# Self attention in a decoder layer: queries scaled at their eviction, row maxima written straight as the exponentials' bias

## The reference

```python
q = (x @ Wq).reshape(b, t, 2 * H, HD).transpose(0, 2, 1, 3) * HD ** (-0.5)   # H = 16, HD = 16: a quarter
k = (x @ Wk).reshape(b, t, 2 * H, HD).transpose(0, 2, 1, 3)
v = (x @ Wv).reshape(b, t, H, 2 * HD).transpose(0, 2, 1, 3)
aw = softmax(einsum('bhqd,bhkd->bhqk', q, k) + causal)
aw = aw.reshape(b, H, 2, t, t);  aw = aw[:, :, 0] - lam * aw[:, :, 1]
attn = einsum('bhqk,bhkd->bhqd', aw, v)      # then an RMS norm over each head and attn @ Wo
```

## Time and profile before

| | us |
|---|---|
| median of 3 runs | 3828.13 |
| lowest, highest | 3823.77, 3829.65 |
| the profiled execution | 3817.57 |
| span of its trace | 3815.8 |

### The profile page before, as it was taken

One profiled execution on the slowest core, in us unless ns is written; L12 is line 12 of the kernel. 1 busy time (PEld: TensorE's weight loads), 2 busy tenths in 40 slices (PEclk: granted clock), 3 DMA queues, 4 the chain that ended last, 5 costly groups with the idle time before them and its releaser, 6 DMA issues.

```text
span 3815.8 us, 74126 instructions
## 1 busy us (share of the span) xinstructions
PE 3668.1 (96%) x24778; PEld 2905.2 (76%) x24778; DVE 2883.4 (76%) x5969; ACT 2352.5 (62%) x5418; POOL 1812.3 (47%) x2121
## 2 busy tenths in 40 slices
PE   6999999789999999999899999999999999999999
PEld 6888888534444444444589999999999999999998
DVE  5888888578888888888457777777777777777333
ACT  5888888457777777777435555555555555555121
POOL 2333332334555555554326666665666665555210
PEclk9999999789999999999899999999999999999999
DMA  5000000133334444443149999999999999998421
GB/s 209 24 25 28 27 26 21 42 108 123 127 124 133 133 128 127 131 154 121 48 141 265 263 268 263 266 268 266 264 267 264 268 265 265 267 262 239 154 84 58
DMA packets 290168, 621.37 MB, mean 163 GB/s; under 512 B 70000, under 2 KB 78576, under 8 KB 289664
## 3 DMA queue, kind: packets, MB, share of 16 engines
q1 hardware_dynamic: 224640, 464.01, 37.1%
q0 software_dynamic: 64000, 150.52, 16.4%
q10 hardware_dynamic: 1152, 2.10, 0.2%
HBM read 459.93 MB, written 155.98 MB: 161 GB/s over the span
## 4 chain that ended last, share of the span: by engine, by line
PE 82%; ACT 7%; DVE 6%; issue 3%; SPq 2%; DMA 1%; POOL 0%; DVEq 0%; ACTq 0%; POOLq 0%
PE ps L620 18%; PE ps L622 17%; PE ps L621 17%; PE ps L804 7%; PE ps L607 4%; PE ps L765 4%; ACT PA L1009 4%; PE ps L787 4%; PE ps L725 2%; PE ps L898 2%; PE ps L924 2%; PE ps L647 2%; ACT PX L1076 1%; DVE NM L1409 1%; DVE WD L1557 1%
## 5 line engine op out<-in xcount | busy, mean ns | idle before, releaser
L620 PE MATMUL ps<-WG,XT 128*128 128x352 f32 x2304 | 765.9, 332 | 7.3 <-DVE XT L1586 4.8
L621 PE MATMUL ps<-WG,XT 128*128 128x352 f32 x2304 | 744.7, 323 | 0.0
L622 PE MATMUL ps<-WG,XT 128*128 128x352 f32 x2304 | 744.6, 323 | 0.0
L1409 DVE TENSOR_REDUCE NM<-ps 128x2 f32<-128x1024 f32 x512 | 614.2, 1217 | 98.9 <-PE ps L765 92.4
L1076 ACT ACTIVATE PX<-ps 128x1024 f32<-128x1024 f32 x512 | 523.4, 1022 | 198.7 <-PE ps L787 184.2
L1903 POOL DMA_INDIRECT sum<-YO,TI x224 | 401.3, 1792 | 488.6 <-issue 393.8
L1222 ACT ACTIVATE HS<-ps 128x352 f32<-128x352 f32 x288 | 133.6, 464 | 561.7 <-PE ps L622 561.7
L1592 DVE TENSOR_TENSOR HS<-ps,HS 128x352 f32<-128x352 f32 x288 | 150.9, 524 | 426.1 <-ACT HS L1222 422.7
L1550 DVE TENSOR_TENSOR WG<-WL,WG 128x704 fp32r<-128x704 f32 x528 | 449.7, 882 | 28.3 <-ACT WG L1189 28.2
L620 PEld LDWEIGHTS ps<-WG,XT 128*128 128x128 f32 x2304 | 434.5, 189 | 9.3 <-DVE XT L1586 6.5
L621 PEld LDWEIGHTS ps<-WG,XT 128*128 128x128 f32 x2304 | 435.0, 189 | 0.0
(11 more groups left out here) (275 smaller groups left out, 8530.8 us busy)
## 6 DMA issues: line engine op xcount, KB each, us to landing
WL<-in_w_gate SPq DMA_DIRECT2D x128, 704.0 KB, 4.2
WL<-in_w_up SPq DMA_DIRECT2D x128, 704.0 KB, 6.0
DL<-in_w_down SPq DMA_DIRECT2D x128, 512.0 KB, 8.4
kq_parts<-HL SPq DMA_DIRECT2D x64, 512.0 KB, 3.0
KS<-kq_parts SPq DMA_DIRECT2D x384, 64.0 KB, 2.3
QS<-kq_parts SPq DMA_DIRECT2D x384, 64.0 KB, 2.4
DL<-in_w_down SPq DMA_DIRECT2D x128, 192.0 KB, 9.2
CB<-sum POOLq DMA_DIRECT2D x64, 256.0 KB, 3.0
```

Of the source, the lines that this page charges most:

```text
L620: pe.matmul(out_, lh(0), rh(0), start=first, stop=False)
L621: pe.matmul(out_, lh(0), rh(1), start=False, stop=False)
L622: return pe.matmul(out_, lh(1), rh(0), start=False, stop=last)
L1409: dve.tensor_reduce(NM[:, g % 2, qc, p:4:2], ps[:, 512 * bk:512 * bk + 1024].rearrange("p (i k) -> p i k", k=512), AX.X, ALU.max, negate=T ...
```

## The change

Both columns of `CST` become a quarter instead of one, so that the evicted queries `qA` and `qB` are a quarter of what they were, and so are the scores. The exponentials take scale 1.0 instead of 0.25. `tensor_reduce` writes its negated maxima straight into the half of the bias tile that `exps` reads, after one wait for the scores and one for the exponentials two units ago. The `tensor_scalar` of L1278 goes (128 instructions), and with it the tile `nm`, the semaphore `v_nm` and the two waits on `v_nb` and `v_nm` on VectorE. The bias tile is now called `nb`. A quarter is a power of two, so the numbers in the exponentials are the same to the last bit except where the format ends.

```diff
-v_na v_nx v_n3 v_xn v_qB v_kT v_nm v_nb v_cc v_aw v_o v_ms v_on v_x1 v_t
+v_na v_nx v_n3 v_xn v_qB v_kT v_nb v_cc v_aw v_o v_ms v_on v_x1 v_t
@@ build
-        nm = sb(ax, "nm", [128, 8])
-        nb4 = sb(ax, "nb4", [128, 2, 8])
+        nb = sb(ax, "nb", [128, 2, 8])
@@ exps, ScalarE
-                    e = act.activation(PA[:, d, h, :], sums[:, h, :], ACT.Exp, bias=nb4[:, d, h:h + 1], scale=0.25,
+                    e = act.activation(PA[:, d, h, :], sums[:, h, :], ACT.Exp, bias=nb[:, d, h:h + 1], scale=1.0,
@@ tops, VectorE
                 dve.wait_ge(S["p_s"], m + 1)
-                if m:
-                    dve.wait_ge(S["v_nb"], m)
-                sums = ps[:, 512 * (1 + 2 * d):512 * (3 + 2 * d)].rearrange("p (h k) -> p h k", k=128)
-                dve.tensor_reduce(nm[:, :], sums, AX.X, ALU.max, negate=True).then_inc(S["v_nm"], 1)
-                dve.wait_ge(S["v_nm"], m + 1)
                 if m >= 2:
                     dve.wait_ge(S["a_e"], m - 1)
-                dve.tensor_scalar(nb4[:, d, :], nm[:, :], 0.25, None, ALU.mult).then_inc(S["v_nb"], 1)
+                sums = ps[:, 512 * (1 + 2 * d):512 * (3 + 2 * d)].rearrange("p (h k) -> p h k", k=128)
+                dve.tensor_reduce(nb[:, d, :], sums, AX.X, ALU.max, negate=True).then_inc(S["v_nb"], 1)
@@ constants
-    c[:, C_AB] = p % 32 < 16
-    c[:, C_AB + 1] = p % 32 >= 16
+    c[:, C_AB] = 0.25 * (p % 32 < 16)
+    c[:, C_AB + 1] = 0.25 * (p % 32 >= 16)
```

## The result

In 20 executions of each kernel the changed kernel takes 3829.36 us (3825.32 to 3834.36) and the kernel before 3823.26 (3818.83 to 3832.23). The ratio is 1.0015, with a 95% interval of 1.0009 to 1.0021, by which it is 5.7 us slower. That is within the 0.2% of "no change", but it is a loss where 0.8 us of gain was forecast. One execution of 6944.3 us, in the first experiment, was in the slow state and is left out of its ratio. The profiled execution of the changed kernel has a span of 3825.8 us, 10.0 more than the one before.

What follows compares the result with a forecast made beforehand. The prediction took TensorE's matmuls and ScalarE's exponentials to bound the self attention. Gains of 0.55 and 0.25 us, with all else zero, made 0.8 us: 3828.1 - 0.8 = 3827.3 us, range 3820 to 3833.

Steps and rivals of the forecast that it cites:

- What bounds the kernel: Self attention: the chain runs through TensorE's matmuls and ScalarE's exponentials, 20.99 us a block, without L1274 or L1278.
- the cover: Self attention half steps: the bias is ready 0.55 us before ScalarE's first exponential, so an earlier bias only lengthens a margin.
- (a): Scaling removed in the self attention: VectorE saves 0.55 us a half step (0.35 to 0.59), 21.9 us of busy time.
- (b): Where VectorE is on the chain: 0.55 us comes through at 132.55 us and 0.25 at 702 to 706, sum 0.8.
- (c): On VectorE the wait for `a_e` moves from the scaling to the reduction; already met, it costs nothing.
- (d): Evictions into `qA` and `qB` keep their form, exponentials take scale 1.0: zero, with a bound of 1.2 us.
- (e): Every tile declared behind `nm` moves down by 32 bytes in SBUF, the experts' weights among them: taken as zero.
- rival C: Experts: the 32-byte shift costs 1 ns more on each expert-weight matmul, 9.5 us lost, 3837 us; chance 4%.
- rival D: Self attention: the reduction really waits for the exponentials two units ago, up to 77 us slower; chance 1%.
- Rival A: Self attention: ScalarE really waits for the bias, so 16 us faster (3812 us) or 35 us (3793); chance 4%.
- Rival B: End of the self attention: a fall of the granted clock goes or comes, 3824 or 3831 us; chance 10% each side.

Runs made afterwards that it cites:

- the first experiment: The changed kernel with an unused tile of 32 bytes a row ahead of nb, so later tiles start where they did before the change; ratio 1.0009 (1.0000 to 1.0019).
- e1: The changed kernel with 32 unused bytes a row ahead of nb, putting later tiles back where they started before the change; ratio 1.0009 (1.0000 to 1.0019), experts 1808.3 us.
- e9: The kernel before with only the down projection tiles WD0 and WD1 at 32 past a multiple of 128 bytes; ratio 1.0012 (1.0002 to 1.0021).
- e8: The kernel before with 32 unused bytes a row ahead of WG0 only, moving just the experts' four weight tiles up; ratio 1.0064 (1.0050 to 1.0078).

## Why the prediction was right or wrong

**What bounds the kernel, and the cover (parts 1 and 2):** right. A block takes 21.00 us with or without the scaling, no wait of ScalarE for the bias came up, and L1273 delays ScalarE once, by 1.0 us at the start. VectorE was busy for 2857.1 us instead of 2883.4, 26 less, where some 22 were named.

**(a), VectorE's own saving:** right, at the upper end. I took 0.55 us a half step with 0.59 as the bound; at the place shown it was 0.60. The distance between the starts of two reductions is 1.14 us, the value that the start 0.09 us ahead of an end had given; in the record above two of them take 2.36 us together. The Trainium skill ("VectorE: DVE Perf Modes", section "The DRAIN you can't avoid") says that the next operation starts only when the pipe is empty, and goes on that one that is not held starts earlier. By the first statement alone, which is all that the prediction took from it, the second start would lie at the first one's end, 1.22 us on. The trace has it 0.08 us sooner, as the second statement allows.

**(b), what comes through:** right, to within 0.1 us. The first place gave 0.60 us where 0.55 was forecast. At the second, TensorE's wait for `norm_o` fell from 2.37 to 1.76 us. ScalarE's copy of `oT` started 3.48 us behind its copy of `awT` before (703.31 to 706.79) and 3.23 after it. So 0.25 us came through there, the value forecast; at the next exponential 0.20 are left. First the copy of `awT` before, then the rows after:

```profile
703.31 0.60 ACT L1017 ACTIVATE awT<-ps 128x512 f32<-128x512 f32 x1 [2.57 <-PE ps L607]
```
```profile
704.40 0.60 ACT L1016 ACTIVATE awT<-ps 128x512 f32<-128x512 f32 x1 [2.56 <-PE ps L606]
706.12 1.12 PE L606 MATMUL ps<-CST,SQ 128*128 128x128 f32 x4 [1.76 <-DVE SQ L1333]
707.63 0.64 ACT L1028 ACTIVATE oT<-ps 128x512 f32<-128x512 f32 x1
```

These are gains in the place where they arise. None can be seen in the whole, since the starts of the cross attention differ by over 1 us between profiles of one kernel.

**(c) and (d):** right. L1273 never waits for the exponentials, and the run with the numbers alone is at 1.0005 (0.9996 to 1.0014).

**(e), the step that failed.** I saw that every later tile moves by 32 bytes, and took zero because two pairs of rows agreed. These rows were no test of what mattered. The rounding was ScalarE's, and the matmuls streamed 32 columns where the experts' stream 352 and 512. I also took it that only odd against even multiples of 32 could count, while the runs show 4.7 us for 96 past a multiple of 128 and 22.7 us for 32, which are both odd multiples. The long, back-to-back matmuls over `WG` and `WD`, on which this stage's time rests, had no row at another start, and the prediction says so itself under rival C. A row that doesn't carry the disputed case bounds nothing. I should have widened the range for it and given rival C, whose mechanism it was, much more than 4%. Its price was twice too high, 9.5 us at 1 ns a matmul. Measured are 4.7 us on its 9504 matmuls, 0.5 ns each. The sign that the prediction names for C, longer matmuls over `WG`, hardly shows in the means. Between 2500 and 2900 us the three lines have 331, 322 and 322 ns before and 333, 323 and 323 after, but the run with the tiles put back (`e1`) has 332, 323 and 323 as well. The count of matmuls in a fixed stretch and the time of 18 steps show it.

The Trainium skill ("SBUF — State Buffer", section "Operand start alignment") says that an operand must start at a multiple of its element size, and that this is a rule of what is allowed and not of speed. Nothing here speaks against that, and the runs give a case in which an allowed start costs time.

**The sum.** 0.8 us of gain was forecast and 5.7 us were lost. The experts' tiles account for 4.7 to 4.8 us. The last 1 us, and what became of the 0.8 us of gain, are below what the runs can tell. With the tiles back the ratios were 1.0009 (1.0000 to 1.0019) and 1.0003 (0.9994 to 1.0012). Among the chances, C's 4% and D's nearly 1% are entered as 4% in all, one too few.

**Rival A** fell with the block's 21.00 us, **rival D** with L1273's missing waits. **Rival B**, the clock, is not shown to have played a part. From 680 to 760 us, the place that the prediction named, the granted clock was 0.66 after and 0.67 before. It differed at the start instead. The second block took 24.87 us after and 23.35 before, with a lower granted clock from 68 to 94 us (0.76 against 0.84, first after, then before):

```profile
68.00:94.00 26.00, 23.19 (x215) 21.15 (x215) 15.62 (x44) 17.26 (x82) 5.73 (x7) 0.76 0.01 2
```
```profile
68.00:94.00 26.00, 23.20 (x224) 21.36 (x223) 17.50 (x50) 18.79 (x90) 5.76 (x7) 0.84 0.01 2
```

The long second block was seen in four of seven profiles of kernels with the change (24.87 to 25.01 us) and in one of seven without (`e9`, 24.90). It is worth 1.5 us. Whether the change makes it more frequent is open.

**The forecast in numbers:** 3827.3 us with 3820 to 3833 was given on a base of 3828.1. The base of 20 executions is 3823.3, so the forecast amounts to 3822.5 against a measured 3829.4. The measured time lies in the range, but only because the base was 4.9 us too high; moved down by as much, the range ends at 3828.1. That is luck. The direction was wrong.

**What stays open:** why matmuls over these tiles take longer from a start at 32 or 96 past a multiple of 128, and why 32 costs five times as much as 96. The runs show the dependence and its place, not its mechanism. VectorE and ScalarE write the same tiles while TensorE reads others of them. ScalarE's writes into `WG` take 789 ns in the mean before and in `e8` and 793 in the changed kernel (2000 to 3450 us), so their length doesn't follow the loss; whether writes and reads meet is not shown. Other operands of TensorE were not moved one by one. The longer cross attention of the first profile after (1060.6 us) was not seen in any of the 13 others (1048.5 to 1054.3 us) and stays unexplained. So the 10.0 us between the first two profiles are more than the change costs.

## What to carry to other kernels

Removing an instruction that lies beside a longer wait gives nothing, and the list of waits says so beforehand. Look for who waits for it, and for what stands ahead of the waiting one. Removing a small tile is a change of its own, since it moves whatever is laid out behind it. Keep the starts of tiles that TensorE streams fixed, by rounding them up or by declaring small tiles last or padded, and when two versions are compared, put a gap where a tile went. Of the four starts tried here, those at 0 and 64 past a multiple of 128 bytes were the good ones.

## What the runs showed of the hardware

The start of a float32r tile that TensorE streams matters at a grain of 32 bytes. With stationary operands and matmuls the same, 594 matmuls of 352 and 512 columns (18 steps, 122.3 or 122.9 us) took 0.30 to 0.33 us more at 96 and 1.42 to 1.44 at 32 past a multiple of 128 bytes than at 0, and 0.13 less at 64. That is 2.4 ns a matmul at worst, at a full granted clock and with TensorE busy for 99.3% of the stretch from 2000 to 3450 us. Over the stage the loss was 4.7 and 22.7 us. ScalarE's exponentials into `PA`, which moved by the same 32 bytes, have a median of 381 ns after and 380 before.
